# Row matrices of a token-mixing kernel loaded from ScalarE's queue in eight transfers per chunk, and column blocks taken in another order

## What is computed

```python
rel = tril(i - j); pos = max(rel.max(-1), |L_multiplier * init_L|)
nd = log(|c * rel| + 1) / (log(|c * pos| + 1) + 1e-6)
y = x + einsum('qkm,mh->hqk', relu(nd[..., None] * W1[0] + b1), W2) + b2
```

```python
out  = einsum('mts,mn->nts', y, w + eye)
out += einsum('its,tin->nts', einsum('mts,tim->its', y, qw1), qw2) + y * qdd[t]
out += einsum('its,sin->nts', einsum('mts,sim->its', y, kw1), kw2) + y * kdd[s]
```

## Time and profile before

| what | us |
|---|---|
| three runs | 990.25, 999.2, 1001.28 (median 999.2) |
| profiled execution, its own time | 1002.05 |
| its span, first to last instruction | 1000.3 |
| first b phase begins | 48.4 |
| a phase of region 0, b phase of region 1 begin | 93.8, 137.9 |
| a phase of the last region begins | 941.5 |

### The profile page before, as it was taken

The page is one execution under the profiler, slowest core; times in us unless marked ns, Lnnn a source line. Parts: engine busy times, 40 slices in busy tenths (PEclk is TensorE's granted clock), DMA queues, the critical chain, the costliest instruction groups (busy, mean ns, idle before and its releaser), DMA issues. The chain is left out here.

```text
span 1000.3 us, 38878 instructions
## 1 busy us (share of the span) xinstructions
PE 757.3 (76%) x18210; PEld 558.0 (56%) x18210; DVE 452.8 (45%) x482; ACT 385.8 (39%) x412; POOL 367.7 (37%) x204
## 2 busy tenths in 40 slices
PE   0678554888879467995889868888898688987962
PEld 0255444666657346764557646656656365756962
DVE  6594422474437333662336515553345343651331
ACT  3878314543545315531443343332343144331100
POOL 3634211332323112342546545563555354740000
PEclk9789776997989879997899999998999799997987
DMA  7795677868895889388854998589937889396089
GB/s 131 175 169 105 132 152 148 157 120 189 190 177 120 185 144 201 76 183 174 178 111 94 195 190 157 97 198 202 167 61 146 191 167 170 66 208 112 15 167 161
DMA packets 360445, 149.62 MB, mean 150 GB/s; under 512 B 93532, under 2 KB 360156, under 8 KB 360284
## 3 DMA queue, kind: packets, MB, share of 16 engines
q1 hardware_dynamic: 222688, 79.98, 43.0%
q10 hardware_dynamic: 137596, 67.14, 30.6%
HBM read 77.61 MB, written 69.47 MB: 147 GB/s over the span
## 5 line engine op out<-in xcount | busy, mean ns | idle before, releaser
L394 POOL TENSOR_TENSOR hidden<-log_table,row_scale 128x1024 f32<-128x1024 f32 x192 | 363.6, 1908 | 525.1 <-PE bias L694 519.4
L430 ACT ACTIVATE hidden<-hidden,b_col 128x1024 f32<-128x1024 f32 x192 | 218.7, 1148 | 335.1 <-POOL hidden L394 182.1
L680 PE MATMUL main<-homes,mats_b 32*32 32x120 f32 (+1 forms) x9216 | 282.7, 272 | 85.7 <-issue 48.7
L680 PEld LDWEIGHTS main<-homes,mats_b 32*32 32x32 f32 x9216 | 257.3, 133 | 151.2 <-issue 96.7
L669 PE MATMUL main<-homes,mats_a 32*32 32x128 f32 x8192 | 273.7, 286 | 88.1 <-DMA mats_a<-a_mats 68.4
L669 PEld LDWEIGHTS main<-homes,mats_a 32*32 32x32 f32 x8192 | 247.6, 132 | 149.2 <-DMA mats_a<-a_mats 76.1
L593 DVE SCALAR_TENSOR_TENSOR homes<-bias,b_col,homes 64x512 f32<-64x512 f32 (+1 forms) x256 | 185.9, 747 | 158.1 <-PE bias L694 94.6
L694 PE MATMUL bias<-hidden,w_blocks 128*64 128x512 f32 x768 | 210.1, 652 | 31.9 <-ACT hidden L430 22.2
L575 DVE TENSOR_TENSOR homes<-main,homes 128x1024 f32<-128x1024 f32 x128 | 156.8, 1225 | 168.4 <-PE main L669 165.2
L565 DVE COPY homes<-main 128x960 f32<-128x960 f32 x64 | 74.1, 1158 | 198.5 <-PE main L680 198.4
L457 ACT ACTIVATE homes<-main 128x960 f32<-128x960 f32 (+1 forms) x80 | 71.1, 891 | 151.7 <-PE main L680 105.4
(11 more groups left out here) (36 smaller groups left out, 29.6 us busy)
## 6 DMA issues: line engine op xcount, KB each, us to landing
out_mixed<-homes ACTq DMA_DIRECT2D x208, 192.0 KB, 5.5
homes<-in_x SPq DMA_DIRECT2D x200, 192.0 KB, 6.8
homes<-in_x SPq DMA_DIRECT2D x72, 256.0 KB, 7.4
out_mixed<-homes ACTq DMA_DIRECT2D x64, 256.0 KB, 6.8
out_mixed<-homes ACTq DMA_DIRECT2D x72, 128.0 KB
homes<-in_x SPq DMA_DIRECT2D x136, 64.0 KB
mats_a<-a_mats SPq DMA_DIRECT2D x64, 128.0 KB
b_mats<-homes SPq DMA_DIRECT2D x2, 512.0 KB, 4.2
```

What stands on the lines that cost most here:

```text
L394: nc.gpsimd.tensor_tensor(hidden_tile(u, g).rearrange("p (j s) -> p j s", j=ROWS), bass.AP(logs.tensor, logs.offset, [list(logs.ap[0]), [1 ...
L430: nc.scalar.activation(hidden_tile(u, g), hidden_tile(u, g), ACT.Relu, bias=b1_col[:, 0:1])\
L680: mm = pe.matmul(main[of_group(g), i % 2, j * W:j * W + REGION_TILES[k] * ROWS], b_weights(g, C * ROWS + j), y_column(k, g, C * ROWS + j), ...
```

## The change

It has three parts. `load_mats_a` moves from SP's program into ACT's; each chunk is now eight transfers, one for each block, of 16 partitions, instead of two of 64; the bytes and the length of the runs stay the same. ACT begins the first two chunks in step 13 of region 0, after a wait for the matrices to be in DRAM, and each later one in the step after the last tile of the chunk it replaces (or in step 0 of the next region), ahead of that step's emptying and relu. SP is left with x, the making of the tables and the final waits. And x loads, stores and row matrices take the blocks in the order 0, 4, 1, 5, 2, 6, 3, 7, where x loads and stores had 0 to 7.

```diff
+BLOCK_ORDER = (0, 4, 1, 5, 2, 6, 3, 7)
...
         def portion_blocks(p):
-            return range(sum(PORTIONS[:p]), sum(PORTIONS[:p + 1]))
+            return BLOCK_ORDER[sum(PORTIONS[:p]):sum(PORTIONS[:p + 1])]
...
-                for b in range(BLOCKS):
+                for b in BLOCK_ORDER:
                     sp.dma_start(home_rows(b, x_slot(k, T), n * ROWS),
                                  x[0, :, t0:t0 + n * ROWS, b * W:(b + 1) * W]).then_inc(x_in[i], DMA)
-
-            def load_mats_a(v):
-                if v >= A_RING:
-                    sp.wait_ge(main_ready, a_tile_of((v - A_RING + 1) * CHUNK_TILES - 1) + 1)
-                slot = v % A_RING
-                for b2 in range(GS):
-                    into = bass.AP(mats_a, (b2 * A_RING + slot) * A_SIZE + b2 * CHUNK,
-                                   [[GS * A_RING * A_SIZE, GROUPS * H], [GS * CHUNK, H], [1, CHUNK]])
-                    sp.dma_start(into, bass.AP(a_mats.tensor, v * H * H * CHUNK,
-                                               [[0, GROUPS], [H * CHUNK, H], [1, H * CHUNK]]))\
-                        .then_inc(a_in[slot], DMA)
...
             sp.wait_ge(mats_out["a"], 2 * DMA)
-            for v in range(A_RING):
-                load_mats_a(v)
             load_x(1, 4)
...
-                    v, last = divmod(tile_of(k, T), CHUNK_TILES)
-                    if last == CHUNK_TILES - 1 and v + A_RING < CHUNKS:
-                        load_mats_a(v + A_RING)
...
+            def load_mats_a(v):
+                if v >= A_RING:
+                    act.wait_ge(main_ready, a_tile_of((v - A_RING + 1) * CHUNK_TILES - 1) + 1)
+                slot = v % A_RING
+                for b in BLOCK_ORDER:
+                    into = of_block(mats_a, A_RING * A_SIZE, b, slot * A_SIZE + b % GS * CHUNK, [[GS * CHUNK, H], [1, CHUNK]])
+                    act.dma_start(into, a_mats[v]).then_inc(a_in[slot], DMA)
...
+                    if s == COL_TILES - 3 and k == 0:
+                        act.wait_ge(mats_out["a"], 2 * DMA)
+                        for v in range(A_RING):
+                            load_mats_a(v)
+
+                    if s > COL_TILES or (s == 0 and k):
+                        v, last = divmod(tile_of(k, s - COL_TILES if s else 0) - 1, CHUNK_TILES)
+                        if last == CHUNK_TILES - 1 and v + A_RING < CHUNKS:
+                            load_mats_a(v + A_RING)
...
-                pe.wait_ge(a_in[v % A_RING], (v // A_RING + 1) * GS * DMA)
+                pe.wait_ge(a_in[v % A_RING], (v // A_RING + 1) * PER_PIECE)
```

## The result

| | us (median, lowest to highest) |
|---|---|
| before, runs beside it | 1000.24 (990.25 to 1001.5) |
| changed | 1068.67 (1060.88 to 1075.16) |
| ratio | 1.071, 95% interval 1.0645 to 1.0779 |

The forecast was 956 with a range to 1012. The time lies outside it, on the side of rival A. On a second chip the changed kernel had a ratio of 1.0753 (1.0643 to 1.0862).

The account below looks back on a forecast made before the run. The prediction took TensorE, busy 757 of 1000 us, to carry the end wherever it doesn't wait; 1002.05 - 6 - 16 - 12 - 5 - 4 = 959 us, 956 against the median. Range 895 to 1012, the forecast's own 930 to 985.

Parts of the forecast that it names:

- rival A: Slower: ACT becomes the bound in the a phases at today's issue price; about 1015 us; chance 0.16.
- Step 1: TensorE's 68.4 us of waits for row matrices go, except perhaps the first chunk's; 62 us of them in seven a phases.
- Step 2: In the a phases ACT's added issues set the pace and make relu late: 52.5 us per phase, -6 us in all.
- the relu term: In ACT's time per a phase: seven relu pairs hold its program some 1.3 us each, 9 us.
- Step 3: At startup x goes out earlier while ACT is held 9.7 us: -6 before region 1, -10 in its b phase.
- Step 4: In the six other b phases x gets ahead by some tiles: -2 us each, -12 us; bounds 0 and -30.
- Step 5: In the last region the 5.75 us wait goes, but 16 issues come between stores: -5 us, bounds +5 and -10.
- Step 6: Block order alternating partition halves for x loads and stores: -4 us, near no effect; bounds 0 and 54 us off.
- B: Rival, much faster: transfer engines relieved, halves overlap, stores at 0.65 us, a phases 49.6 to 46 us; 900 us; chance 0.25.

## Why the forecast was wrong

**Step 1** (the waits for matrices go) was right for the seven a phases, where 1.7 us of 62 are left. The other 8.4 of the 10.1 us are two waits in the last region, one of 5.4 us, above the 2 us that the forecast had set as its sign. Its reason was half right. It took the gain mainly from the form and named the place behind x beside it. The run with eight transfers on SP kept 47 of 68 us, so the place was two thirds; the run that put the matrices first bears this out (40.3 to 5.5 us). And 62 us of gain was too much: the run without later loads on SP shows that only some 29 us could be had from all of it.

**Step 2** (what ACT pays) is the step that failed. It had the mechanism: it said that ACT sets the pace and relu comes late. It forecast 52.5 us per a phase, at most 60; measured were 436.0 / 7 = 62.3, and 39.5 in place of 33.7 us for the last b phase. Three terms of its sum were mis-sized:

| per a phase | forecast | changed kernel, mean of the seven |
|---|---|---|
| until the first store | 5.2 | 7.1 |
| stores | 32 x 0.72 = 23.0 | 27.6 (0.85 each) |
| row-matrix issues | 24 x 0.608 = 14.6 | 22.3 (25 x 0.89) |

The row-matrix issue was priced from eight issues on a queue with nothing else to do, and this is the largest miss, 7.7 us. The store was taken near its median, against a sample of 0.96; its mean in the a phases was 0.91 before and 0.85 in the changed kernel, so the reason given for the low price, that stores would speed up once the chunk's 13 us had gone, had a small effect. The first store stood 7.8 us into the phase already in the rows at hand (526.00 in rows 6, 533.81 in rows 8). With the measured terms and the sum's 9 us of relus it gives 66.0 us, 3.7 above the 62.3 found; the relu term is then too large, or part of it runs beside issues. A sum wants means.

The sum also left out the order of the work in ACT's program. The issues come in one block of eight behind a portion of stores, so the relu is late even where ACT has time left on average: ACT was issuing for 49.9 of the 62.3 us. And it had no term for the lower clock behind late relus, which goes with the 15.1 us by which TensorE's busy time grew in the a phases.

**Step 3** (startup: -6 before region 1, -10 in its b phase) came out at -0.1 and -6.2 (63.2 to 57.0 us). ACT's hold in step 13 was 12.5 us, not 9.7, but the run that moved it to SP won only 1.3 us at this point, with x later in exchange. What the b phase of region 1 waited for in all three traces is x behind the first stores.

**Step 4** (the other b phases, -12) was +11: regions 2 and 3 won 3.5 and 2.8 us, regions 4, 6 and 7 lost 5.7, 2.3 and 9.3. There the relu is late too: TensorE waited 5.8, 4.9 and 9.0 us for it in these three, against 2.2, 2.8 and 2.2 before. This is the sign that the forecast had named for the whole being wrong, b phases that lengthen by ACT's backlog.

**Step 5** (-5): the last a phase with its tail took 58.5 us against 58.8. The wait of 5.75 us did not go: TensorE waited 3.0 and 5.4 us for the matrices there. The loads stood between the stores.

**Step 6** (the order) was mis-sized the other way. It took -4, near no effect; the order alone gave -33 us. Its reason for a small price was that all engines of a transfer write one half; that neighbouring transfers overlap after all would explain the gain, but no run shows it. The Trainium skill's two statements can now be weighed. By the rule not to bother with transfers to different halves (DMA: Bandwidth & Descriptors, Rules for kernel authors) the order gives 0; here, for a queue of block transfers, it gave 3.3% of the time and 11% of the engine time on SP's queue, so the measurement decides against the rule. The port count of SBUF - State Buffer (The DMA port swizzle) leaves room for a gain, but the rate of x loads alone stayed near 204 GB/s, so that the ports are the cause is not shown.

**The rivals.** A was the right one and got 0.16. Its point of decision was given as 56.5 us per phase; by the forecast's own numbers, 53.3 + 37/7, it is 58.6, and the phases stood 4 us above even that. So A was weighed against a wrong threshold. Its time of 1015 rested on -37 us from the other steps, which were worth about nothing: 1002 + 63 for the a phases + 5 for the seven b phases + 6 for the last one gives 1076 for a like execution. B was wrong: stores took 0.85 us where it had 0.65, and x loads alone did not rise above 204 GB/s by much. The forecast's test for A, ACT issuing throughout a phases of 60 us, is near what the trace shows: 49.9 of 62.3 us.

## What to carry to other kernels

An engine that feeds the bottleneck pays for a transfer's issue in full, and in one piece: price it with the mean of its issues in the stretch where it will stand, not with the median or with that of a quiet queue. Before moving transfers, ask what stands behind them in the new program and when it is due; a wait of 68 us for data was cheaper here than a queue that holds the relu. Where transfers touch disjoint partition ranges and their order is free, try the order by itself first: it cost three lines and was the only part of this change that gained time by itself (3.3%).

## What the runs showed that I had not expected

- Eight issues of a sixteenth of the data held ACT for 6.5 to 7.1 us, about as long as the full ones in a phase of the changed kernel (6.8 to 7.9). Over the whole runs they took 0.82 against 0.90 us each. The hold hardly follows the bytes of the transfer being issued. Whether it follows what is under way on the queue ahead of it was not separated.
- Two transfers in place of eight held ACT for 2.9 to 12.2 us per chunk, 6.2 in the mean, and made the stores behind them slower as well: 1.16 us in the mean against 0.92.
- The order of the blocks cut the engine time of the same packets on SP's queue by 11% in the kernel before. With the loads on ACT it cut it by 6%, and nothing is shown for ACT's queue.
- Waits of TensorE for nothing that the profile shows were 45 to 74 us in the column products of every variant, and grew where others shrank. The traces tell more about them. One queue carries packets of a kind of its own, in the kernel before:

```profile
q8 instruction: 143, 2.34, 1.2%
```

These 2.34 MB are about 64 bytes for each of the 36420 matmuls and weight loads, so they look like TensorE's own program. In the kernel before, all 23 of its unexplained waits over 1 us ended 1.2 to 2.0 us after such a packet had landed; of the 25 other waits over 1 us two did, and at a random time the chance is 0.12. In the changed kernel it was 25 of 28, against 1 of 32. So most of these waits look like waits for instructions, which come over the transfer engines: in the 2 us ahead of such a wait and in it, their busy share was 1.00 in the mean, against 0.75 over the run. This is a coincidence in time, read from the packets one by one, and no run changed it on purpose.
